# Convolution attention by query halves: weighted sum of two key tiles in one bank, output stored by halves, maxima turned two tiles later

## The reference

```python
qh, kh, vh = ...          # (8 images, 8 heads, 1024 positions, 8)
logits  = einsum('bnid,bnjd->bnij', qf, kf) + rel_w + rel_h   # relative position terms in x and y
weights = softmax(logits, axis=-1)
attn    = einsum('bnij,bnjd->bnid', weights, vf)
```

## Time and profile before

| what | value |
|---|---|
| time, median of three runs (lowest, highest) | 2469.61 us (2463.07, 2480.05) |
| the profiled execution: its time, its span | 2465.86 us, 2464.0 us |
| PE busy / DVE busy / ACT busy over the span | 2184.8 / 1342.1 / 1214.7 us |
| mean granted TensorE clock | 0.934 |
| first and last score (line 907) of the main block | 646.7, 1478.8 us |
| first-pass reductions (line 644) in all | 512, mean 1219 ns |
| exponentials (line 882) | 1024, mean 596 ns |
| last POOL split of expert weights (line 861) | starts at 1077.2 us |

### The profile page before, as it was taken

How to read it: one execution, slowest core, us unless ns; L and a number is a source line. 1 busy time by engine, 2 the same in 40 slices (tenths; PEclk the granted TensorE clock), 3 DMA queues, 4 the chain that set the end, 5 groups by cost and what they waited for, 6 DMA issues and landing times. The chain is left out here.

```text
span 2464.0 us, 32921 instructions
## 1 busy us (share of the span) xinstructions
PE 2184.8 (89%) x10534; PEld 1511.8 (61%) x10534; DVE 1342.1 (54%) x2054; ACT 1214.7 (49%) x2160; POOL 272.7 (11%) x258
## 2 busy tenths in 40 slices
PE   4999999946999999999999983888888893999997
PEld 3777888745545444454455431677777772888886
DVE  6232333124777667677777712466565652566665
ACT  2121222121467666667677771555555552566664
POOL 1000000000122222210000002212122200000000
PEclk9999999955699999999999996999999996999999
DMA  2322243396777678776567203322322114444531
GB/s 72 98 64 64 65 139 122 131 202 197 210 160 168 147 160 164 165 143 105 91 112 121 42 9 101 117 90 93 98 98 90 51 52 156 149 146 139 210 128 60
DMA packets 154696, 291.40 MB, mean 118 GB/s; under 512 B 32448, under 2 KB 94656, under 8 KB 150464
## 3 DMA queue, kind: packets, MB, share of 16 engines
q1 hardware_dynamic: 145568, 263.83, 41.6%
q0 software_dynamic: 7680, 25.17, 3.6%
q10 hardware_dynamic: 1312, 0.67, 0.1%
HBM read 179.69 MB, written 107.25 MB: 116 GB/s over the span
## 5 line engine op out<-in xcount | busy, mean ns | idle before, releaser
L644 DVE TENSOR_REDUCE a_nmax<-a_sm 128x1 f32<-128x1024 f32 x512 | 604.0, 1219 | 229.7 <-PE a_sm L664 229.5
L882 ACT ACTIVATE p_shared<-a_st 128x512 f32<-128x512 f32 x1024 | 556.6, 596 | 264.4 <-PE a_st L907 262.9
L922 PE MATMUL a_pv<-p_shared,a_va 128*32 128x512 f32 x2048 | 276.5, 613 | 0.9 <-ACT p_shared L882 0.9
L664 PE MATMUL a_sm<-a_kf,a_qf 120*128 120x512 f32 x704 | 218.7, 429 | 62.6 <-DMA a_kf<-kq_d 38.3
L907 PE MATMUL a_st<-a_qf,a_kf 121*128 121x512 f32 x704 | 257.5, 444 | 17.7 <-ACT p_shared L882 8.0
L907 PEld LDWEIGHTS a_st<-a_qf,a_kf 121*128 121x128 f32 x704 | 121.1, 192 | 220.4 <-ACT p_shared L882 198.3
L1797 PE MATMUL x_h_ps<-x_v_hi,x_w 128*128 128x512 f32 x512 | 180.8, 395 | 25.4 <-DVE x_v_lo L1738 25.4
L664 PEld LDWEIGHTS a_sm<-a_kf,a_qf 120*128 120x128 f32 x704 | 136.6, 204 | 100.7 <-issue 32.6
L1811 PE MATMUL x_y_ps<-x_h_hi,x_w 128*128 128x512 f32 x512 | 178.0, 389 | 0.0
L1748 DVE SCALAR_TENSOR_TENSOR x_h_lo<-x_hid,x_wts,x_h_hi 128x512 fp32r<-128x512 f32 x128 | 96.0, 750 | 138.0 <-ACT x_h_hi L1719 138.0
L1715 ACT ACTIVATE x_hid<-x_h_ps,x_b 128x512 f32<-128x512 f32 x128 | 88.4, 691 | 130.6 <-PE x_h_ps L1797 125.7
(11 more groups left out here) (248 smaller groups left out, 3615.2 us busy)
## 6 DMA issues: line engine op xcount, KB each, us to landing
x_w<-w_d SPq DMA_DIRECT2D x32, 1024.0 KB, 8.5
rel_d<-p_shared SPq DMA_DIRECT2D x12, 2048.0 KB, 12.2
a_qf<-rel_d SPq DMA_DIRECT2D x44, 512.0 KB
a_qf<-rel_d SPq DMA_DIRECT2D x44, 256.0 KB
p_q_all<-rel_d SPq DMA_DIRECT2D x20, 512.0 KB
a_qf<-kq_d SPq DMA_DIRECT2D x66, 128.0 KB
c_xtok<-in_x SPq DMA_DIRECT2D x8, 1024.0 KB, 5.7
va_d<-c_va SPq DMA_DIRECT2D x16, 512.0 KB, 4.8
```

The lines of the kernel that those rows point to most:

```text
L644: nc.vector.tensor_reduce(nmax[:, h, t:t + 1], sm[k % 2][:], axis=AX.X, op=ALU.max, negate=True).then_inc(sm_read, 1)
L664: m = nc.tensor.matmul(sm[k % 2][:, cols], qf[j][0:ROW_M, h, half, t * P:(t + 1) * P], kf[j][0:ROW_M, h, cols], start=True, stop=True)
L882: nc.scalar.activation(probs[:, t % 2, h, half * HALF:(half + 1) * HALF], st[half][:], ACT.Exp).then_inc(exp_done, 1)
L922: m = nc.tensor.matmul(pv[32 * h:32 * h + 32, cols], va[j][:, t, h, :], probs[:, t % 2, h, cols], start=t == 0, stop=t == TT - 1, skip_gro ...
```

## The change

It does seven things. (1) A query half is finished for all its key tiles before the other half begins: scores and exponentials of a period now run half, key tile, head. (2) `pv` is one bank, for one half at a time; ScalarE copies half 0 out in the middle of its own period (after exponential 39 of 64) and half 1 after the eighth exponential (u = 7) of the next. (3) PE's order is written out in `ORDER`, for a batch of eight scores (s), eight first-pass matmuls (m) and two `weighted` (v), which are two key tiles of one half, next to each other; a period is eight batches. (4) `st` has three banks, `probs` four slots. (5) `sm` is four single banks; each reduction covers 512 logits, and for each pair of heads VectorE takes the smaller of the two halves' negated maxima after a drain. (6) The turn of a pair of heads stands behind the second tile of the next head, so the second turn of a period comes in batch 7 (the last), behind its fourth m, and SP sends maxima in two parts. (7) SP stores halves: in period n first half 1 of group n - 1, then `load(n + 2)`, two heads' maxima, half 0 of group n, the other two heads' maxima. The d = 1 tiles begin with the first m of batch 7. The block ahead uses the same halves.

```diff
+        SB = 4
+        sm = [ctx.enter_context(nc.psum_tensor(f"a_sm{i}", [P, HALF], f32)) for i in range(SB)]
...
         def first_pass_units(whole):
             units, step = [], 0
             for d, h, t in [(0, h, t) for h in range(HG) for t in range(TT)][AHEAD:] + [(1, 0, t) for t in range(AHEAD) if whole]:
-                if t == 0 and h % 2 == 0:
-                    units.append((step, "turn", 0, (h - 1) % HG, 0))
-                units.append((step, "logits", d, h, t))
-                step += 1
-            return units if whole else units + [(step, "turn", 0, HG - 1, 0)]
+                units.append((step, "logits", d, h, t, 0))
+                units.append((step + 1, "logits", d, h, t, 1))
+                if t == 1 and h % 2 == 0:
+                    units.append((step + 1, "turn", 0, (h - 1) % HG, 0, 0))
+                step += 2
+            return units if whole else units + [(step, "turn", 0, HG - 1, 0, 0)]
         first_pass_of = {whole: first_pass_units(whole) for whole in (True, False)}
...
+        slots = {"logits": 1, "turn": 2}
...
+        STEPS = 2 * TT * HG
+        NS = STEPS
+        STB = 3
+        SLOTS = 4
+        BATCH = 2 * HG
+        NB = NS // BATCH
+        ORDER = "mssmsmsvvsmsmmsmsm"
...
-        def maxima(sp, n, j, whole):
-            for h in range(HG):
+        def maxima(sp, n, j, whole, first):
+            for h in (first, first + 1):
                 for half in range(2):
                     if half == 0:
-                        sp.wait_ge(sm_read, units_before(n) + unit_at[whole]["turn", 0, h | 1, 0] + 1)
+                        sp.wait_ge(sm_read, units_before(n) + slot_at[whole]["turn", 0, h | 1, 0, 0] + 2)
                     sp.dma_start(bits(qf[j][:])[ROW_M:ROW_M + 1, h, half, :].rearrange("a (t p) -> a t p", p=P),
                                  bits(mrow[h % 2 * TT:(h % 2 + 1) * TT, h // 2, :])).then_inc(max_loaded[h], 16)
-        def logits_max(dve, before, k, h, t):
+        def logits_max(dve, before, k, h, t, half):
             dve.wait_ge(sm_done, before + k + 1)
-            nc.vector.tensor_reduce(nmax[:, h, t:t + 1], sm[k % 2][:], axis=AX.X, op=ALU.max, negate=True).then_inc(sm_read, 1)
+            nc.vector.tensor_reduce(nmax_half[:, half, h, t:t + 1], sm[k % SB][:], axis=AX.X, op=ALU.max, negate=True).then_inc(sm_read, 1)
+            if h % 2 and t == TT - 1 and half:
+                dve.drain()
+                nc.vector.tensor_tensor(nmax[:, h - 1:h + 1], nmax_half[:, 0, h - 1:h + 1], nmax_half[:, 1, h - 1:h + 1], ALU.min
+                                        ).then_inc(nmax_ready, 1)
...
         def logits(pe, j, before, k, h, t, half):
-            if half == 0 and not (isinstance(before, int) and before + k < 2):
-                pe.wait_ge(sm_read, before + k - 1)
+            if not (isinstance(before, int) and before + k < SB):
+                pe.wait_ge(sm_read, before + k + 1 - SB)
             cols = slice(half * HALF, (half + 1) * HALF)
-            m = nc.tensor.matmul(sm[k % 2][:, cols], qf[j][0:ROW_M, h, half, t * P:(t + 1) * P],
-                                 kf[j][0:ROW_M, h, cols], start=True, stop=True)
-            if half == 1:
-                m.then_inc(sm_done, 1)
...
+                    pe.wait_ge(sm_read, units_before(n) + k + 1 - SB)
+                    pe.wait_ge(nmax_ready, n * (HG // 2) + (h + 1) // 2)
+                    nc.tensor.transpose(sm[k % SB][0:2 * TT, 0:P], nmax[:, h - 1:h + 1, :].rearrange("p h t -> p (h t)"), ident[:]).then_inc(sm_done, 2)
...
-        probs = bits(shared[:])
+        probs = bits(shared[:]).rearrange("p a h n -> p (a h n)").rearrange("p (t h n) -> p t h n", t=SLOTS, h=HG)
         out = sb("a_out", [P, TOK])
-        st = [ctx.enter_context(nc.psum_tensor(f"a_st{i}", [P, HALF], f32)) for i in range(2)]
-        pv = ctx.enter_context(nc.psum_tensor("a_pv", [P, TOK], f32))
+        st = [ctx.enter_context(nc.psum_tensor(f"a_st{i}", [P, HALF], f32)) for i in range(STB)]
+        pv = ctx.enter_context(nc.psum_tensor("a_pv", [P, HALF], f32))
...
                 def period(n, j, more, ahead):
+                    if not (isinstance(n, int) and n == 0):
+                        store(n - 1, 1)
                     if ahead:
                         load(n + 2, (j + 2) % BUFS)
-                    if not (isinstance(n, int) and n == 0):
-                        store(n - 1)
                     if more:
-                        maxima(sp, n + 1, (j + 1) % BUFS, ahead)
-                def store(n):
-                    sp.wait_ge(out_ready, n * 2 + 4)
-                    sp.dma_start(att_d.rearrange("b g p n -> (b g) p n")[n], out[:]).then_inc(out_stored, 16)
-                sp.sem_inc(out_stored, 16)
+                        maxima(sp, n + 1, (j + 1) % BUFS, ahead, 0)
+                    store(n, 0)
+                    if more:
+                        maxima(sp, n + 1, (j + 1) % BUFS, ahead, 2)
+                def store(n, half):
+                    cols = slice(half * HALF, (half + 1) * HALF)
+                    sp.wait_ge(out_ready, n * 2 + half + 3)
+                    sp.dma_start(att_d.rearrange("b g p n -> (b g) p n")[n, :, cols], out[:, cols]).then_inc(out_stored[half], 16)
...
                 def copy_out(n, half):
-                    cols = slice(half * HALF, (half + 1) * HALF)
-                    act.wait_ge(pv_done, n * 2 * TT + 2 * TT + 3 + half)
-                    if half == 0:
-                        act.wait_ge(out_stored, n * 16 + 16)
-                    nc.scalar.activation(out[:, cols], pv[:, cols], ACT.Copy).then_inc(out_ready, 1)
+                    act.wait_ge(pv_done, n * 2 * TT + TT * (half + 1) + 4)
+                    act.wait_ge(out_stored[half], n * 16 + 16)
+                    nc.scalar.activation(out[:, half * HALF:(half + 1) * HALF], pv[:], ACT.Copy).then_inc(out_ready, 1)
                 def period(n, j, more, ahead):
                     for u in range(NS):
-                        t, h, half = u // (2 * HG), u // 2 % HG, u % 2
                         act.wait_ge(st_done, n * NS + u + 1)
-                        if h == half == 0:
-                            act.wait_ge(pv_done, n * 2 * TT + 2 * t + 2)
-                        nc.scalar.activation(probs[:, t % 2, h, half * HALF:(half + 1) * HALF], st[half][:], ACT.Exp
-                                             ).then_inc(exp_done, 1)
-                        if u in (3, 7) and not (isinstance(n, int) and n == 0):
-                            copy_out(n - 1, u // 4)
+                        if u % BATCH == 0:
+                            act.wait_ge(pv_done, n * 2 * TT + 2 * (u // BATCH) + 2)
+                        nc.scalar.activation(probs[:, u // HG % SLOTS, u % HG], st[(j + u) % STB][:], ACT.Exp).then_inc(exp_done, 1)
+                        if u == BATCH - 1 and not (isinstance(n, int) and n == 0):
+                            copy_out(n - 1, 1)
+                        if u == NS // 2 + BATCH - 1:
+                            copy_out(n, 0)
                 all_groups(act, period)
-                for half in range(2):
-                    copy_out(NG - 1, half)
+                copy_out(NG - 1, 1)
...
-                def scores(n, j, s, half):
-                    t, h = s // HG, s % HG
-                    pe.wait_ge(exp_done, n * NS + 2 * s + half + 1)
-                    if t == half == 0:
+                def scores(n, j, u):
+                    half, t, h = u // (TT * HG), u // HG % TT, u % HG
+                    pe.wait_ge(exp_done, n * NS + u + 1)
+                    if u < HG:
                         pe.wait_ge(max_loaded[h], n * 32 + 32)
-                    nc.tensor.matmul(st[half][:], kf[j][0:ROW_M + 1, h, t * P:(t + 1) * P],
+                    nc.tensor.matmul(st[(j + u) % STB][:], kf[j][0:ROW_M + 1, h, t * P:(t + 1) * P],
                                      qf[j][0:ROW_M + 1, h, 2 * t // TT, half * HALF:(half + 1) * HALF],
                                      start=True, stop=True).then_inc(st_done, 1)
-                def weighted(n, j, t, half):
-                    if half == 0:
-                        pe.wait_ge(exp_done, n * NS + 2 * HG * (t + 1) + 2)
-                    if t == half == 0:
+                def weighted(n, j, w):
+                    half, t = w // TT, w % TT
+                    pe.wait_ge(exp_done, n * NS + HG * (w + 1) + STB)
+                    if w == 0:
                         pe.wait_ge(loaded[j], times_loaded(n, j))
                     if t == 0:
-                        pe.wait_ge(out_ready, n * 2 + half + 1)
-                    cols = slice(half * HALF, (half + 1) * HALF)
+                        pe.wait_ge(out_ready, n * 2 + half + 2)
                     for h in range(HG):
-                        m = nc.tensor.matmul(pv[32 * h:32 * h + 32, cols], va[j][:, t, h, :], probs[:, t % 2, h, cols],
```

(64 more changed lines are left out.)

37 lines of the change are left out of this document (16 added, 21 removed).

## The result

The changed kernel took 2568.8 us (median of 4, 2554.1 to 2570.6) against 2466.3 for the kernel before (2459.6 to 2480.1): a ratio of 1.0395, 95% interval 1.0335 to 1.0455 (it is not the quotient of the two medians, which is 1.0416). Forecast were 2560 us and a range of 2495 to 2605. The profiled execution's span is 2568.9 us against 2464.0.

A forecast was written before the change was run, and what follows sets the result against it. PE's period and the load chain bound it within 2 us of each other. Thirteen load-bound steps, 61.7 us with POOL's weights and 58.4 without, add 98.8; tail -4, block ahead 0 to +2: +95, 2560 us, range 2495 to 2605.

The forecast's parts named there:

- The load starts later: In SP's queue the load stands behind the waiting store of half 1: landing to issue 15.7 us instead of 9.1.
- The store's bytes: 256 KB ahead of the load in the DMA queue cost 0 to 2.5 us; 1.7 taken.
- The load's length: A load takes 39.3 us without POOL's weights beside it, 42.6 with them, before 1.7 for the store's bytes.
- The maxima's wait: Second turn behind batch 7's fourth m: the next period's score u = 3 waits 2.4 us for its maxima.
- The clock: Half clock behind PE's waits for loads: 1.7 us added per step, bounded by 0 and twice that.
- The joined products: Two `weighted` in a row save 0.40 us a pair: batches of 5.80 us, 3.2 less over eight.
- The tail: Behind the last load: period 14 saves about 1 us, period 15 up to 6, period 13's batch 7 costs 3.5; together -4.
- (a): At batch 7's first m loads don't decide and PE's saving shows: -41 us, 2425 us; chance 4%.
- (b): Loads bind, but store bytes, clock and half of the maxima's wait cost nothing: -60, 2500 us; chance 20%.
- (c): Cancels: L, a load's length, falls to 35 us in the quiet half as well as (b): 2471 us; chance 6%.
- (d): Clock at 1.2 GHz twice as long, VectorE reductions 0.75 us: +29, 2590 us; chance 18%.
- (e): Joined products write one bank and wait for each other: 0.3 us a step, inside the range; no chance given.

The follow-up runs named there:

- e8: Kernel before, with queries and keys of each load issued once the scores reading the buffer are through, values last at the old wait: 2454.8 us, ratio 0.9951.
- e5: Kernel before, with the relative terms (8 of 18 DMAs, 3.0 of 4.6 MB) left out of loads from group 3 on: 2453.3 us, ratio 0.9942.
- e6: Changed kernel, with the relative terms (8 of 18 DMAs, 3.0 of 4.6 MB) left out of loads from group 3 on: 2454.0 us, ratio 0.9939.
- e7: Changed kernel with load ahead of store, turn behind the next head's first tile, and queries and keys loaded early: 2453.8 us, ratio 0.9937.
- e4: Changed kernel, SP still waiting for ScalarE's copy of half 1 but issuing the load before the store: 2562.0 us, ratio 1.0404.
- e1: Changed kernel with load(n + 2) put ahead of the store of half 1 in SP's order: 2497.6 us, ratio 1.0156.
- e12: Changed kernel with a new ORDER alone, mssmsmsmvvsmssmmsm: 2545.2 us, ratio 1.0327.
- e11: Changed kernel with load ahead of store and queries and keys loaded early, turns and ORDER as in the change: 2455.8 us, ratio 0.9952.
- e2: Changed kernel with the turn behind the first tile of the next head instead of the second: 2546.7 us, ratio 1.0325.
- e9: Changed kernel with load ahead of store, queries and keys loaded early, turns as changed, and ORDER mssmsmsmvvsmssmmsm: 2438.5 us, ratio 0.9881.
- e3: Changed kernel with the load ahead of the store and the turn behind the next head's first tile: 2474.4 us, ratio 1.0046.

## Why the prediction was right, step by step

- **What bounds the kernel.** Right. The two limits lay close: with the loads out of the way the kernel before gains 13 us (e8) or 15 (e5), and the changed one 115 (e6, e7).
- **The load starts later.** Right, and the largest term: landing to issue was forecast at 15.7 plus 1.7 for the clock, 17.4. Nine steps show 17.2 to 18.8; four show 20.3 to 22.8, and the mean is 18.9. Three of those four follow the loop boundaries, where e8 too has steps of 55.0 to 56.4 beside 50.3: stalls which the sum held on its before side only, in the 680.8 (landing to issue there is 10.4 in the mean, not 9.1). The fourth, 20.9, is the step from 939.79: its maxima's wait is 2.0 us, and the clock falls a second time, so that the granted clock from landing to issue is 0.77 and 4.7 us are lost to it.
- **The store's bytes.** Mis-sized: 1.7 us forecast, at most about 0.4 found (e4). Its issue was put at 0.5, and e4's steps are 0.4 shorter. The Trainium skill, DMA: Bandwidth & Descriptors, Queues, rings and completion order, where each engine takes a ring's descriptors in order, put the term at its upper end, 2.5; these runs show no such price for 256 KB, and the measurement decides.
- **The load's length.** 41.0 forecast with the store's bytes, 44.3 with POOL's weights. In the changed kernel it is 41.8 over the five loads beside POOL's splits, whose last write is issued at 1023.9, and 40.9 over the eight behind them, 41.3 in all where 42.6 was forecast. Over the six kernels after, e1 to e4 and e12 the means are 42.3 and 40.7. So POOL's price is 1.6 us (0.5 to 3.1 by kernel) and not 3.3, and the quiet length was put at 39.3 where 40.7 was due, which the bytes hid. 1.3 us a step too much here, 17 us, made up for the stalls and the clock.
- **The maxima's wait.** 2.4 forecast, too dear: about 1.4 in e11. The fourth score comes 2.6 to 3.0 us into most quiet periods of the changed kernel instead of 1.2 to 1.4 without a wait (e2, e9), so 1.2 to 1.8 behind a landing. e2 has 12 us less in the 13 steps, with its own waits at the turns in them.
- **The clock.** 1.7 a step forecast. The 13 windows of 7 us behind landings grant 0.67 on average: 7 x 0.33 = 2.3 us. From landing to the next load's issue it is 2.9 us in the mean, and 2.4 without the three steps at the loop boundaries. The Trainium skill, TensorE: Matmul & The Clock Gate, HAM oscillation, by which each wait puts the next burst at half clock, agrees: all 14 landings show it, that behind a wait of 3.6 us too. The wait of 1.7 us in the earlier trace rows and the one of 1.4 us in e1, behind which a first-pass matmul took 0.49 us and not 0.79, did not.
- **PE's wait for keys.** Forecast at 8 to 12 us a step, measured 6.6 over the 13 steps (6.8 with the wait ahead of them). A step is PE's own period, the clock and the wait: 50.3 + 2.3 + 6.6 = 59.2, which leaves 1.0 for the stalls at the loop boundaries. The forecast took less for the first two.
- **The joined products.** A pair takes 1.92 us as forecast and a plain batch 5.90 instead of 5.80. PE's own period was forecast at 49.8 and is 50.14 in e11. The saving of 3.2 is real but for those 0.1 in each plain batch, and waits give it back.
- **The tail.** Forecast -4, measured +3.6. Period 14 takes 50.3 us against 49.6 before, where a microsecond less had been forecast. From the last landing to period 14 it takes 9.5 us instead of 4.2, 5.4 more where 3.5 had been forecast; 3.1 of them are half clock. Period 15 saves 2.4 of the 6 held possible. The granted clock has the rest, as the rows below this list show.
- **The rivals.** (a) is out: its place was right, but e5 to e8 show that even with short or early loads the change brings nothing over the kernel before with the same loads, so its 41 us were not to be had with this ORDER. (b) was right for the bytes alone; the clock is paid in full, and more than half of the maxima's wait. (c) is out, no load of the changed kernel took under 38.4 us. (d) is out as a whole, with part of its clock term true (2.4 to 2.9 us lost a step, between the forecast's 1.7 and its 3.4): reductions take 0.683 us each and 0.61 back to back, not 0.75. (e) is out by the 1.92.

Period 15 from its first to its last score, in the changed kernel and in e6, whose period 15 is the same program (columns as in the earlier trace rows):

```profile
1538.88:1586.06 47.18, 44.45 (x193) 14.83 (x192) 0.00 (x0) 32.69 (x66) 0.00 (x0) 0.93 0.03 12
1422.19:1466.10 43.91, 41.18 (x192) 14.48 (x191) 0.00 (x0) 32.69 (x66) 0.00 (x0) 1.00 0.03 13
```

ScalarE is equally busy in both, and 47.2 us at 0.93 are about 3.3 us of lost clock. Nothing shows why the clock fell there: no load is in flight, and PE has only short waits for exponentials in both.

**The sum.** 779.6 us were forecast for the 13 steps and 782.9 measured, so the mechanism was right, and that the size fits within 4 us in 780 is in part luck, by errors against each other: the store's bytes, the maxima's wait and POOL's weights were too dear, the stalls, the quiet load and the clock too cheap.

**What stays open.** No run holds the clock fixed, so the split of e1's gain between the earlier issue (3.6 us a step) and the spared clock (1.4) is read from one pair of traces. Why the clock fell in period 15 is not shown. Nor is it shown why batches of one period differ by 0.2 us, 5.90 beside 6.11; ScalarE's copy is the suspect, and only argued.

## What to carry to other kernels

Before moving an instruction in a queue, read what is queued behind it: here the wait of a small store held back a load on which the next period hung, and that cost some 60 to 70 of 102 us, its bytes next to nothing. When a loop has two limits within 2 us of each other, compute the length of the other one first; a saving on PE can then bring little, and a delay of the other is paid in full every period. And a saving inside a period shows only if nothing else in it waits: the new order of the units, together with the early load, was needed before the joined products paid.

## What the runs showed of the hardware

- A 256 KB store issued 0.7 us ahead of a load of 4.6 MB in the same queue lengthened it by 0.4 us at most: 41.3 us against 41.2 in e4, 41.6 against 41.2 over three kernels each.
- The same load's time from issue to use spreads from 38.4 to 44.5 us over the 13 steps of the changed kernel, and both ends of that spread lie behind POOL's traffic. Of the two values of the earlier trace rows, 42.6 and 44.8, the second is outside it; POOL's price is 1.6 us as a mean of six kernels.
- Reductions of 128x512 from PSUM follow each other every 0.61 us, and two joined products, 16 column-strip matmul instructions, take 1.92 us, as at the end of the block before the change.
- Behind a wait of 3.6 us the next 7 us were granted 0.76 of the clock and behind 7.1 us 0.58; behind 1.4 us (e1) the matmuls ran at their full-clock length. The length of the wait alone does not decide it: behind one of 2.4 us in e1 the next 7 us were granted 0.76, behind one of 3.1 us in e3 1.00.
- The clock can fall without a long wait: period 15 of the changed kernel, where PE is 94% busy, was granted 0.93 on average and took 47.2 us; the same period in e6 was granted 1.00 and took 43.9.
